# A transformer layer on one core: the first attention group's tiles filled on chip, and its shift rows written directly

## The chip, the cores and the metric

One core of a Trainium2 chip. The metric is the device time of one execution in microseconds (us). TensorE is PE in the profile, VectorE is DVE, ScalarE is ACT, GpSimd is POOL, SyncE is SP; PEld are TensorE's weight loads, and a q behind an engine (SPq, ACTq) marks its issues of DMAs.

## The reference

```python
# x: (2, 1024, 128) float32; 16 heads of two sub-heads each, HD = 4
def sdpa(qi, ki):
    s = jnp.einsum('bnhd,bmhd->bhnm', qi, ki) * scale
    p = jax.nn.softmax(s, axis=-1)
    return jnp.einsum('bhnm,bmhe->bhne', p, v)
o = sdpa(q0, k0) - lam * sdpa(q1, k1)        # differential attention
o = rms_norm(o, sub_norm_w) * (1.0 - LAMBDA_INIT)
...
x = x + attn_a(layernorm(x))    # the above, with w_qkv, w_proj, b_proj
x = x + ffn(layernorm(x))       # 64 experts, top 8 of them, and a shared one
x = x + attn_b(layernorm(x))    # attention among the 16 heads, summed over the sequence
x = x + ffn(layernorm(x))
```

## The kernel before

**Queries and keys.** The tokens are 4 chunks of 512 (`NCH`), two for each of the 2 batches. For a chunk VectorE and GpSimd make the norm, TensorE transposes, ScalarE copies the result to `XT`, and TensorE makes a tile of queries and one of keys. Each is split into three bf16 parts (`PARTS`): ScalarE copies the high part, VectorE subtracts it into `R1` (the remainder), ScalarE copies the middle part, VectorE subtracts again for the low part. A product of scores is one bf16 matmul over 32 rows: 6 pairs of parts (`Q_SLOTS`, `K_SLOTS`) of 4 elements, and 8 more rows of which three carry the shift of the softmax for each query against ones in the keys.

**The stacks.** SyncE writes these rows to DRAM (`q_stack`, `k_stack`), 14 transfers for each batch, and reads them back as tiles: a group is 4 sub-heads in 4 strips of 32 partitions, 16 groups in all (`NG`). `QB` and `KB` hold a group for the scores, `QA` and `KA` hold it for the max pass with the two halves of the keys in different strips. Each is double-buffered (u).

**The attention.** It runs in 256 quads (`NQ`), 16 for a group. A quad has four score matmuls, their four exps on ScalarE (`PR`, line 858), 16 matmuls of `PR` with the values (`VG`, line 1358) and two items of the max pass: two matmuls with 1024 keys (line 1294), and the maximum over them by VectorE (line 1065) into `NEGMAX`. The max pass runs `LEAD` = 12 quads ahead, so the first 24 items stand alone. After the 16 items of a half group GpSimd splits the 16 shifts of each partition into three bf16 parts (`SHP`, `shift_parts`), TensorE transposes them in the quad that is 3 before the half group's first scores, VectorE copies them to `SHT`, SyncE writes them to `shift_d` in DRAM and then in four transfers to `QB` (`shift_rows`). A score's bank is one of three (4 to 6), an item's two of four (0 to 3), bank 7 sums the values. `OTS` and `OSB` are the sums on their way out once in a half group.

**The weights of the experts.** `RAWU` and `RAWD` are loaded on ScalarE's queue, 2 MB each; ScalarE makes the high parts (`WUH`, `WDH`), GpSimd the low ones (`WUL`, `WDL`, line 628). The last quads overlap with the experts' beginning, after which eight passes (a chunk each, twice) over 16 groups of four experts and the shared one follow. `PR` lies over `PARTS`, so that the first exp waits for all writes of the stacks.

Each engine works through its own list in order; semaphores alone connect them. The order is written by hand.

## Time and profile before

| | |
|---|---|
| time, median of 3 runs | 1091.02 us (1089.59 to 1094.71) |
| the profiled execution | 1090.65 us |
| its span | 1088.8 us |
| VectorE busy | 959.6 us (88%) |
| TensorE busy | 1001.9 us (92%) |
| ScalarE busy | 890.0 us (82%) |
| GpSimd busy | 485.9 us (45%) |

The span goes from the first to the last instruction; the rest of the time lies around it. Busy times are sums over the span, and the stages differ: they are read by window. In brackets behind an instruction stands the idle time ahead of it and what ended it.

### The profile page before, as it was taken

The page shows a single profiled execution, that of the slowest core. Times are in us where ns is not written, and L with a number is a line of the kernel's source. Part 1 is how long each engine was busy: PE and PEld are TensorE (multiplying, and loading weights), DVE is VectorE, ACT ScalarE, POOL GpSimd, SP SyncE. Part 2 cuts the span into 40 slices and gives each one's busy share as a digit, 9 for nine tenths or more (in the row PEclk, how much of TensorE's full clock was granted, in tenths as well). Part 3 has the DMA queues.
Part 4 walks back from the last instruction along what each step waited for, and adds up shares of the span by engine and source line. Part 5 has one row for each costly group of instructions (what it writes and reads, how often), then busy time and mean ns, then how long its engine had stood idle before and what let it go on. Part 6 is the DMA issues. An engine that isn't in the chain of part 4 may idle for free.

```text
span 1088.8 us, 21671 instructions
## 1 busy us (share of the span) xinstructions
PE 1001.9 (92%) x8016; PEld 515.6 (47%) x8016; DVE 959.6 (88%) x1186; ACT 890.0 (82%) x1466; POOL 485.9 (45%) x893
## 2 busy tenths in 40 slices
PE   6389999999999999999999999999899999999998
PEld 3022222222222222222222236787677777777876
DVE  7799999999999999999999947798866988787665
ACT  5179999999999999999999987777775787678765
POOL 3363555455555544564556467342413431323331
PEclk9579999999999999999999999999999999999999
DMA  8911110111011101100110008575757466757763
GB/s 277 304 30 50 52 51 4 50 51 51 4 51 51 37 17 51 51 26 28 52 51 22 3 8 192 144 187 131 173 150 179 136 160 179 194 145 182 197 190 90
DMA packets 80473, 108.91 MB, mean 100 GB/s; under 512 B 23536, under 2 KB 33520, under 8 KB 80368
## 3 DMA queue, kind: packets, MB, share of 16 engines
q1 hardware_dynamic: 66336, 100.98, 34.4%
q10 hardware_dynamic: 14032, 6.55, 2.3%
q8 instruction: 64, 1.05, 0.4%
q14 instruction: 41, 0.34, 0.1%
HBM read 95.57 MB, written 11.93 MB: 99 GB/s over the span
## 4 chain that ended last, share of the span: by engine, by line
DVE 54%; PE 27%; ACT 7%; issue 6%; DMA 5%; POOL 1%; SPq 1%; ACTq 0%; DVEq 0%; POOLq 0%
DVE NEGMAX L1065 46%; PE PS L1456 7%; PE PS L1458 7%; PE PS L1457 7%; PE PS L1358 2%; DVE HF L1106 2%; DVE HL L1114 2%; ACT PR L858 2%; DMA GATE<-gate_d 1%; PE PS L1331 1%; ACT PS L955 1%; ACT HH L948 1%; ACT L955 1%; DVE ln_st L1000 1%; DMA shift_d<-SHT 1%
## 5 line engine op out<-in xcount | busy, mean ns | idle before, releaser
L1065 DVE TENSOR_REDUCE NEGMAX<-PS 128x1 f32<-128x1024 f32 x512 | 584.6, 1208 | 10.4 <-PE PS L1294 9.7
L858 ACT ACTIVATE PR<-PS 128x512 f32<-128x512 f32 x1024 | 538.9, 600 | 37.1 <-PE PS L1331 24.2
L1358 PE MATMUL PS<-PR,VG 128*32 128x256 f32 (+1 forms) x3840 | 321.3, 406 | 17.3 <-ACT PR L858 2.0
L1331 PE MATMUL PS<-QB,KB 32*128 32x512 bf16 x1024 | 260.1, 387 | 3.7 <-DMA QB<-shift_d 2.5
L1294 PE MATMUL PS<-KA,QA 32*128 32x512 bf16 x1024 | 204.3, 397 | 31.2 <-DVE NEGMAX L1065 22.4
L1106 DVE TENSOR_TENSOR HF<-PS,GATE 128x1024 f32<-128x1024 f32 x128 | 156.2, 1221 | 72.7 <-ACT PS L955 62.3
L1331 PEld LDWEIGHTS PS<-QB,KB 32*128 32x128 bf16 x1024 | 75.0, 91 | 239.8 <-ACT PR L858 137.4
L955 ACT ACTIVATE PS<-PS 128x1024 f32<-128x1024 f32 x128 | 129.2, 1010 | 71.5 <-PE PS L1458 70.9
L948 ACT ACTIVATE HH<-HF 128x1024 fp32r<-128x1024 f32 (+1 forms) x136 | 139.8, 1029 | 34.4 <-DVE HF L1106 32.6
L770 POOL TENSOR_TENSOR HL<-HF,HH 128x1024 fp32r<-128x1024 f32 (+1 forms) x32 | 69.2, 2162 | 165.8 <-ACT HH L948 165.8
L1358 PEld LDWEIGHTS PS<-PR,VG 128*32 128x32 f32 x3840 | 76.4, 108 | 130.7 <-issue 64.6
L1114 DVE TENSOR_TENSOR HL<-HF,HH 128x1024 fp32r<-128x1024 f32 x104 | 131.5, 1265 | 7.6 <-ACT HH L948 7.5
L1456 PE MATMUL PS<-XH,WUH 128*128 128x512 f32 x256 | 107.4, 420 | 0.0
L1456 PE MATMUL PS<-HH,WDH 128*128 128x512 f32 x256 | 103.1, 403 | 3.0 <-ACT YS L965 2.5
L1458 PE MATMUL PS<-HH,WDL 128*128 128x512 f32 x256 | 101.8, 398 | 0.0
L1457 PE MATMUL PS<-HL,WDH 128*128 128x512 f32 x256 | 101.3, 396 | 0.0
L1457 PE MATMUL PS<-XL,WUH 128*128 128x512 f32 x256 | 101.2, 395 | 0.0
L1458 PE MATMUL PS<-XH,WUL 128*128 128x512 f32 x256 | 101.0, 394 | 0.0
L676 POOL TENSOR_TENSOR ORC<-OSB,MINUS 128x16 f32<-128x16 f32 x32 | 93.2, 2911 | 3.3 <-DVE OSB L1091 0.9
L642 POOL TENSOR_TENSOR SHP<-NEGMAX,ZERO 128x16 bf16<-128x16 f32 x32 | 7.0, 218 | 167.5 <-DVE NEGMAX L1065 167.5
L1294 PEld LDWEIGHTS PS<-KA,QA 32*128 32x128 bf16 x1024 | 48.3, 91 | 59.4 <-DVE NEGMAX L1065 45.3
L1456 PEld LDWEIGHTS PS<-HH,WDH 128*128 128x128 f32 x256 | 48.6, 190 | 16.6 <-ACT YS L965 4.7
(186 smaller groups left out, 970.1 us busy)
## 6 DMA issues: line engine op xcount, KB each, us to landing
GATE<-gate_d SPq DMA_DIRECT2D x256, 256.0 KB, 4.1
QA<-q_stack SPq DMA_DIRECT2D x64, 128.0 KB, 2.6
QB<-q_stack SPq DMA_DIRECT2D x16, 256.0 KB, 2.9
KB<-k_stack SPq DMA_DIRECT2D x16, 256.0 KB, 3.0
KA<-k_stack SPq DMA_DIRECT2D x60, 64.0 KB, 2.4
q_stack<-PARTS SPq DMA_DIRECT2D x12, 256.0 KB, 4.4
k_stack<-PARTS SPq DMA_DIRECT2D x12, 256.0 KB, 4.6
RAWU<-in_L_ffn_W_up_dram ACTq DMA_DIRECT2D x4, 512.0 KB, 13.0
```

Of the source, the lines that this page charges most:

```text
L858: nc.scalar.activation(PR[:, s % PRING, r, :], PS[:, SCORE_BANK[n], :], ACT.Exp, scale=SCALE_A).then_inc(p_ready, 1)
L948: nc.scalar.activation(HH[:, k, 0:u, :], HF[:, f, 0:u, :], ACT.Copy).then_inc(hh_ok, 1)
L955: nc.scalar.activation(PS[:, z:z + 2, :], PS[:, z:z + 2, :], ACT.Silu).then_inc(silu_ok, 1)
L1065: nc.vector.tensor_reduce(NEGMAX[:, hs % 2, col:col + 1], PS[:, e:e + 2, :].rearrange("p b n -> p (b n)"), axis=AX_X, op=ALU.max, negate=T ...
L1106: nc.vector.tensor_tensor(HF[:, k, :, :], PS[:, z:z + 2, :], GATE[:, h % GSLOTS, :, :], op=ALU.mult).then_inc(hf_ok, 1)
L1114: nc.vector.tensor_tensor(HL[:, k, 0:u, :], HF[:, f, 0:u, :], HH[:, k, 0:u, :].bitcast(F32), op=ALU.subtract).then_inc(hl_ok, 1)
L1294: last = mm(PS[:, e + h, :], QA[lo:lo + STRIP, u, r // 2, nt * P:(nt + 1) * P], KA[lo:lo + STRIP, u, r // 2, :], start=True, stop=True)
L1331: mm(PS[:, SCORE_BANK[n], :], KB[strip, u, mt * P:(mt + 1) * P], QB[strip, u, half * BANK:(half + 1) * BANK], start=True, stop=True).then_ ...
L1358: last = mm(PS[STRIP * r:STRIP * (r + 1), 7, cols], VG[:, u, mt, r // 2, :], PR[:, s % PRING, r, cols], start=mt == 0, stop=mt == TB - 1 a ...
L1456: mm(dst, ah, bh, start=first, stop=False)
L1457: mm(dst, ah, bl, start=False, stop=False)
L1458: return mm(dst, al, bh, start=False, stop=last)
```

## The change

Group 0 of the attention no longer takes the way over DRAM: `QB` and `KB` are set to 0 and 1 by VectorE at the start, and 12 transfers (`first_rows`) write the parts of the first four sub-heads from `PARTS` into them. To make rows of one slot lie 8 partitions apart, the order of the 32 rows is now element by slot (`HD_A`, `SLOTS`). The max pass of group 0 reads `QB` and `KB`, both halves of the keys in one strip, and starts when these transfers have landed. The values' matmuls, before in one piece ahead of the max pass, stand one tile behind each of its items 1 to 16, and the centroids behind item 17; they use banks 4 to 6. The loads of `QA`/`KA` for group 0 are gone.

The first batch's parts are made in another order, with four buffers for the remainder and some low parts on GpSimd. TensorE runs 4 and 6 matmuls without use (`warm`) at the start. The writes of the stacks are 8 for a batch, those with several slots in one transfer. The small products of `lam` move from VectorE to GpSimd, X+BPROJ to its half group 3.

A shift row takes one transfer from `SHT` to `QB` (`shift_rows`); the transposed tile has a fourth, zero part, 64 partitions for 48. The load of `RAWU` goes to SyncE in 16 pieces behind the shift rows of groups 0 to 7, `WUH` is made in 8 pieces of 512 columns at quads 28, 44, ... 140, `WUL` in 8 pieces at half groups 6, 8, ... 20.

```diff
...
+SLOTS = STRIP // HD_A
+SHIFT_SLOT = SLOTS - 1
+STACK_WRITES = 16 * 2 * 4
+FIRST_LOADS = 16 * 2 * len(Q_SLOTS)
...
+A_LATE = A_ITEM["va", 0]
+def a_bank(n):
+    return n % 4 if n < A_LATE else 4 + (n - A_LATE) % 3
...
+UP_PIECES = 8
+UP_PARTS = 2 * UP_PIECES
+def up_piece(s):
+    k = (s - 28) // QPG
+    return k if s >= 28 and (s - 28) % QPG == 0 and k < UP_PIECES else None
...
+            load_x(0)
+            load_x(1)
+            sp.dma_start(WQKV[:], w_qkv.rearrange("(j p) c -> p j c", p=P)).then_inc(ld_w, 16)
+            sp.dma_start(WPRJ[:], w_proj).then_inc(ld_w, 16)
+            load_x(2)
+            load_x(3)
+            sp.wait_ge(const_ok, 2)
...
+                    step = places[1] - places[0] if len(places) > 1 else 1
+                    rows = stack[b * GPB:(b + 1) * GPB].rearrange("g r d c n -> (g r d) c n")[:, places[0]:places[-1] + 1:step, :]
+                    sp.dma_start(rows, src.unsqueeze(1).to_broadcast([P, len(places), SEQ])).then_inc(st_w[b], 16)
+            def first_rows(part):
+                for tile, j, slots in ((QB, 0, Q_SLOTS), (KB, 1, K_SLOTS)):
+                    for c in [c for c, a in enumerate(slots) if a == part]:
+                        sp.dma_start(tile[c:P:SLOTS, 0, :], PARTS[0:R * HD_A, part, j, 0:SEQ]).then_inc(first_ld, 16)
...
+            sp.wait_ge(first_set, 2)
+            for part, made in enumerate((qk_hi, qk_mid)):
+                sp.wait_ge(made, 2 * NCH // BATCH)
+                first_rows(part)
+            sp.wait_ge(qk_lo_pool, 2)
+            sp.wait_ge(qk_lo, 2)
+            first_rows(2)
+            for part in range(3):
+                write_parts(0, part)
+            fill_shift_rows(1)
+            for part, (made, n) in enumerate(((qk_hi, 2 * NCH), (qk_mid, 2 * NCH), (qk_lo_pool, 6))):
+                sp.wait_ge(made, n)
+                write_parts(1, part)
...
             sp.wait_ge(st_w[0], STACK_WRITES)
-            load_max(0, 0, False)
+            load_max(1, 1)
+            sp.wait_ge(const_ok, 3)
             sp.dma_start(RAWSU[:, 0:F], ws_up).then_inc(ld_exp, 16)
             sp.dma_start(RAWSD[0:F, :], ws_down).then_inc(ld_exp, 16)
-            fill_shift_rows(1)
-            write_stacks(1)
-            load_max(1, 1)
             sp.wait_ge(st_w[1], STACK_WRITES)
...
             def shift_rows(s, half):
                 u, hs = s % 2, 2 * s + half
+                if half == 0 and s:
+                    sp.wait_ge(sh_w, 16 * s)
                 sp.wait_ge(sht_ok, hs + 1)
-                sp.dma_start(shift_d[half].rearrange("a r (t n) -> (a r t) n", n=P), SHT[:, half, :]).then_inc(sh_w, 16)
-                sp.wait_ge(sh_w, 48 * s + 16 * (half + 2))
-                for r in range(R):
-                    lo = STRIP * r + SHIFT_ROW
-                    sp.dma_start(QB[lo:lo + 3, u, half * BANK:(half + 1) * BANK], shift_d[half, :, r, :]).then_inc(sh_r, 16)
+                sp.dma_start(QB[SHIFT_SLOT:P:SLOTS, u, half * BANK:(half + 1) * BANK], SHT[:, half, :]).then_inc(sh_r, 16)
...
                 for half in range(2):
                     shift_rows(s, half)
+                    if s < UP_PIECES:
+                        load_up(2 * s + half)
...
+            def low_part(c):
+                cols = slice(c * BANK, (c + 1) * BANK)
+                for j in range(2):
+                    n = D_ITEM["qk", j, c]
+                    pool.wait_ge(qk_mid, n + 1)
+                    nc.gpsimd.tensor_tensor(PARTS[:, 2, j, cols], R1[:, n % 4, :], PARTS[:, 1, j, cols], op=ALU.subtract).then_inc(qk_lo_pool, 1)
             for c in range(NCH):
                 root_of(("a", c))
+            for c in (0, 2, 3):
+                low_part(c)
...
+            def low_up(k):
+                cols = slice(k * BANK, (k + 1) * BANK)
+                low_weights(3 + k, WUL[:, cols], RAWU[:, cols], WUH[:, cols])
...
+            link(nc.gpsimd.memset(ZERO[:], 0.0))
+            link(nc.gpsimd.memset(SHP[:], 0.0))
             link(nc.gpsimd.memset(VG[:], 0.0))
             link(nc.gpsimd.memset(VG[:, :, :, :, VD:VD + 1], 1.0))
+            low_weights(0, WDL[:], RAWD[:], WDH[:])
+            pool.wait_ge(ld_mix, 16 * 9)
+            for j in range(2):
+                link(nc.gpsimd.tensor_tensor(lam_p[:, j, :], LAM[:, 2 * j, :], LAM[:, 2 * j + 1, :], op=ALU.mult))
+            link(nc.gpsimd.tensor_tensor(lam_p[:, :, 0:2], lam_p[:, :, 0:2], lam_p[:, :, 2:4], op=ALU.add))
+            nc.gpsimd.tensor_tensor(lam_s[:], lam_p[:, :, 0], lam_p[:, :, 1], op=ALU.add).then_inc(lam_in, 1)
+            link(nc.gpsimd.tensor_scalar(SUBW[:], SUBW[:], 1.0 - LAMBDA_INIT, None, ALU.mult))
+            shift_parts(0)
             values(0, 0)
             values(1, 1)
...
+                if hs == 3:
+                    pool.wait_ge(ln_xn, NCH)
+                    nc.gpsimd.tensor_tensor(X[:], X[:], BPROJ[:].unsqueeze(1).to_broadcast([P, NT, DIM]), op=ALU.add).then_inc(xb_ok, 1)
+                if hs >= 6 and hs % 2 == 0 and hs // 2 - 3 < UP_PIECES:
+                    low_up(hs // 2 - 3)
...
+            transposed(0)
+            high_part(0, 0)
+            transposed(1)
+            high_part(1, 0)
+            middle_part(0, 0)
+            high_part(0, 1)
+            middle_part(1, 0)
+            high_part(1, 1)
+            transposed(2)
+            middle_part(0, 1)
+            middle_part(1, 1)
+            transposed(3)
+            for c in range(2, NCH):
                 for j in range(2):
-                    n = D_ITEM["qk", j, c]
-                    act.wait_ge(d_full, n + 1)
-                    nc.scalar.activation(PARTS[:, 0, j, cols], PS[:, 4 + n % 4, :], ACT.Copy).then_inc(qk_hi, 1)
+                    high_part(j, c)
                 for j in range(2):
-                    n = D_ITEM["qk", j, c]
-                    act.wait_ge(qk_r1, n + 1)
-                    nc.scalar.activation(PARTS[:, 1, j, cols], R1[:, n % 2, :], ACT.Copy).then_inc(qk_mid, 1)
+                    middle_part(j, c)
+            act.wait_ge(ld_down, 16)
+            nc.scalar.activation(WDH[:], RAWD[:], ACT.Copy).then_inc(w_hi, 1)
             for c in range(NCH):
-                evac(("xT", c), XT[:, c * BANK:(c + 1) * BANK], lambda n: PS[:, n, :])
-                if c:
-                    high_and_middle(c - 1)
-            high_and_middle(NCH - 1)
-            for c in range(NCH):
-                b, h = c // 2, c % 2
-                evac(("va", c), VALL[:, b * GPB:(b + 1) * GPB, h * 4:(h + 1) * 4, :].rearrange("p g t v -> p t g v"),
-                     lambda n: PS[:, n, :].rearrange("p (t g v) -> p t g v", t=4, g=GPB))
+                values(c)
...
+            act.wait_ge(first_ld, FIRST_LOADS)
             for b in range(BATCH):
...
+            def high_up(k):
+                cols = slice(k * BANK, (k + 1) * BANK)
+                act.wait_ge(ld_up, 16 * UP_PARTS // UP_PIECES * (k + 1))
+                nc.scalar.activation(WUH[:, cols], RAWU[:, cols], ACT.Copy).then_inc(w_hi, 1)
...
+                if up_piece(s) is not None:
+                    high_up(up_piece(s))
...
+            def rest(j, c):
+                n = D_ITEM["qk", j, c]
+                dve.wait_ge(qk_hi, n + 1)
+                if n >= 4:
+                    dve.wait_ge(qk_mid, n - 3)
+                    if n < 6:
+                        dve.wait_ge(qk_lo_pool, n - 3)
+                    else:
+                        dve.wait_ge(qk_lo, n - 5)
+                nc.vector.tensor_tensor(R1[:, n % 4, :], PS[:, 4 + n % 4, :], PARTS[:, 0, j, c * BANK:(c + 1) * BANK],
+                                        op=ALU.subtract).then_inc(qk_r1, 1)
...
+            nc.vector.memset(QB[:, 0, :], 0.0).then_inc(first_set, 1)
+            nc.vector.memset(KB[:, 0, :], 1.0).then_inc(first_set, 1)
             for c in range(NCH):
                 dve.wait_ge(ld_x[c], 16)
                 stats(("a", c))
                 if c:
                     norm(("a", c - 1))
+            rest(0, 0)
+            rest(1, 0)
             norm(("a", NCH - 1))
-            for c in range(NCH):
-                rest_and_low(c)
-            dve.wait_ge(ld_mix, 16 * 9)
-            for j in range(2):
-                link(nc.vector.tensor_tensor(lam_p[:, j, :], LAM[:, 2 * j, :], LAM[:, 2 * j + 1, :], op=ALU.mult))
-            nc.vector.tensor_reduce(lam_s[:], lam_p[:], axis=AX_X, op=ALU.add).then_inc(lam_in, 1)
-            link(nc.vector.tensor_scalar(SUBW[:], SUBW[:], 1.0 - LAMBDA_INIT, None, ALU.mult))
+            rest(0, 1)
+            rest(1, 1)
+            low_part(0, 1)
+            low_part(1, 1)
...
+            for c in range(2, NCH):
+                rest(0, c)
+                rest(1, c)
...
-                nc.vector.tensor_copy(SHT[:, hs % 2, :], PS[0:3 * SHIFTS, SCORE_BANK[n], 0:P // 2].bitcast(BF16)).then_inc(sht_ok, 1)
+                    dve.wait_ge(sh_r, 16 * (hs - 1))
+                nc.vector.tensor_copy(SHT[:, hs % 2, :], PS[0:4 * SHIFTS, SCORE_BANK[n], 0:P // 2].bitcast(BF16)).then_inc(sht_ok, 1)
...
+            def warm(times):
+                for _ in range(times):
+                    mm(PS[:, 7, :], identb[:], ONES[:, 0:BANK], start=True, stop=True)
             pe.wait_ge(ident_ok, 1)
+            pe.wait_ge(identb_ok, 1)
+            pe.wait_ge(const_ok, 2)
+            warm(4)
...
+            def late_value(i):
+                c, j = divmod(i, 4)
+                n, t = A_ITEM["va", c], i
+                if i == 0:
+                    pe.wait_ge(qk_r1, 2 * NCH)
+                if j == 0 and n - A_LATE >= 3:
+                    pe.wait_ge(a_free, n - 2)
+                last = mm(PS[:, a_bank(n), j * P:(j + 1) * P], XT[:, t * P:(t + 1) * P], WT[:, 2, :], start=True, stop=True)
+                if j == 3:
+                    last.then_inc(a_full, 1)
+            def centroids():
+                n = A_ITEM["centT"]
+                pe.wait_ge(ld_b, 16 * 5)
+                pe.wait_ge(a_free, n - 2)
+                nc.tensor.transpose(PS[:, a_bank(n), 0:E], CENT[:], ident[0:E, 0:E])
+                nc.tensor.transpose(PS[:, a_bank(n), E:E + DIM], WB[:, 2, :], ident[:]).then_inc(a_full, 1)
+            warm(6)
+            transposed(0)
+            copied(0)
+            query_or_key(0, 0)
+            transposed(1)
+            query_or_key(1, 0)
+            copied(1)
+            query_or_key(0, 1)
+            query_or_key(1, 1)
+            transposed(2)
+            transposed(3)
+            for c in range(2, NCH):
+                copied(c)
+                query_or_key(0, c)
+                query_or_key(1, c)
+            pe.wait_ge(first_ld, FIRST_LOADS)
...
+                    if ga == 0:
+                        strip = slice(STRIP * r, STRIP * (r + 1))
+                        for h in range(2):
+                            last = mm(PS[:, e + h, :], QB[strip, 0, nt * P:(nt + 1) * P],
+                                      KB[strip, 0, h * BANK:(h + 1) * BANK], start=True, stop=True)
+                        last.then_inc(m_full, 1)
+                        if 1 <= it <= TOK // P:
+                            late_value(it - 1)
+                        elif it == TOK // P + 1:
+                            centroids()
+                        continue
...
+                    pe.wait_ge(sh_r, 16 * (s // TB + 1))
...
+                if s == 9 - LEAD:
+                    pe.wait_ge(a_free, len(A_ITEM))
...
```

## Rows read from the trace of the kernel before

**Rows 1.** The page: the chain by line, and the score matmuls in the table of groups.

```profile
DVE NEGMAX L1065 46%; PE PS L1456 7%; PE PS L1458 7%; PE PS L1457 7%; PE PS L1358 2%; DVE HF L1106 2%; DVE HL L1114 2%; ACT PR L858 2%; DMA GATE<-gate_d 1%; PE PS L1331 1%; ACT PS L955 1%; ACT HH L948 1%; ACT L955 1%; DVE ln_st L1000 1%; DMA shift_d<-SHT 1%
...
L1331 PE MATMUL PS<-QB,KB 32*128 32x512 bf16 x1024 | 260.1, 387 | 3.7 <-DMA QB<-shift_d 2.5
```

**Rows 2.** Table by stage: window; its length, busy time of each engine; granted clock, DMA share, GB/s.

```profile
36.60:62.00 25.40, 13.21 (x45) 2.37 (x45) 25.40 (x24) 4.11 (x4) 11.65 (x11) 0.50 0.90 276
62.00:70.00 8.00, 7.59 (x38) 1.25 (x36) 7.12 (x7) 5.12 (x10) 8.00 (x3) 0.51 0.00 1
...
670.00:1088.80 418.80, 395.38 (x1802) 316.24 (x1800) 327.59 (x509) 299.50 (x335) 135.86 (x123) 0.99 0.63 162
```

**Rows 3.** Timeline of the beginning: start, length over all instructions of the group, engine, line.

```profile
12.29 1.11 DVE L1012 TENSOR_SCALAR XC<-X,ln_mv,ln_inv 128x128 f32<-128x128 f32 x4
...
12.90 1.80 SPq L495 DMA_DIRECT2D EBIAS<-L_ffn_expert_biases_dram  x1
...
13.89 0.60 ACT L812 ACTIVATE PARTS<-PS 128x512 bf16<-128x512 f32 x1 [1.11 <-PE PS L1247]
...
15.69 1.28 DVE L1022 TENSOR_TENSOR SQ<-PS,PARTS 128x512 f32<-128x512 f32 x2
...
17.14 1.29 DVE L1027 TENSOR_TENSOR PARTS<-SQ,PARTS 128x512 bf16<-128x512 f32 x2 [0.17 <-ACT PARTS L816]
...
19.12 1.95 SPq L480 DMA_DIRECT2D q_stack<-PARTS  x3
...
23.02 3.73 PE L1253 MATMUL PS<-WT,XT 128*128 128x128 f32 x32
...
36.60 21.58 DVE L1065 TENSOR_REDUCE NEGMAX<-PS 128x1 f32<-128x1024 f32 x19 [7.66 <-PE PS L1294]
```

**Rows 4.** Timeline of VectorE, 60 to 690 us.

```profile
69.37 8.04 DVE L1065 TENSOR_REDUCE NEGMAX<-PS 128x1 f32<-128x1024 f32 x7 [0.88 <-PE PS L1294]
...
77.46 18.27 DVE L1065 TENSOR_REDUCE NEGMAX<-PS 128x1 f32<-128x1024 f32 x16
...
95.77 18.27 DVE L1065 TENSOR_REDUCE NEGMAX<-PS 128x1 f32<-128x1024 f32 x16
...
610.63 14.88 DVE L1065 TENSOR_REDUCE NEGMAX<-PS 128x1 f32<-128x1024 f32 x13
```

**Rows 5.** Chain of waits, 26 to 100 us: start, length, what.

```profile
26.35 2.75 DMA k_stack<-PARTS
...
31.20 4.62 DMA KA<-k_stack
```

**Rows 6.** Groups of instructions from 36 to 62 us.

```profile
L1294 PE MATMUL PS<-KA,QA 32*128 32x512 bf16 x48 | 14.0, 602 | 20.6 <-DVE NEGMAX L1065 12.2 <-DMA KA<-k_stack 8.3
...
L628 POOL TENSOR_TENSOR WDL<-RAWD,WDH 128x4096 fp32r<-128x4096 f32 x1 | 8.8, 8809 | 20.9 <-ACT WDH L839 20.9
```

**Rows 7.** Timeline from 55 to 80 us, SyncE's issues of the first shift rows.

```profile
59.72 1.20 SPq L536 DMA_DIRECT2D QB<-shift_d  x4
```

**Rows 8.** Tile SHT from 40 to 110 us: its writes to shift_d.

```profile
DMA to landing us min/median/max: 1.3/1.3/1.4
```

**Rows 9.** Tile PARTS up to 60 us: its writes to the stacks.

```profile
DMA to landing us min/median/max: 2.5/4.4/7.0
```

**Rows 10.** Timeline from 168 us: a score and a pair of the max pass.

```profile
168.05 0.39 PE L1331 MATMUL PS<-QB,KB 32*128 32x512 bf16 x1
168.05 0.39 PE L1294 MATMUL PS<-KA,QA 32*128 32x512 bf16 x2
```

**Rows 11.** Waits of TensorE, 60 to 680 us: in total, times, longest.

```profile
PE PS L1331 <- DMA QB<-shift_d: 2.5, 6, 0.9
```

**Rows 12.** Timeline of ScalarE, 124 to 164 us.

```profile
158.38 0.59 ACT L869 ACTIVATE OTS<-PS 128x512 f32<-128x512 f32 x1
158.86 1.58 ACT L858 ACTIVATE PR<-PS 128x512 f32<-128x512 f32 x3
```

**Rows 13.** Timeline of GpSimd, 100 to 180 us.

```profile
147.43 0.22 POOL L642 TENSOR_TENSOR SHP<-NEGMAX,ZERO 128x16 bf16<-128x16 f32 x1 [3.17 <-DVE NEGMAX L1065]
```

More of the change, by code:

```diff
@@ L365, in hybrid_layer @@
         OTS = sb("OTS", [P, 2, BANK], where=attn)
-        SHP = sb("SHP", [P, 2, 3 * SHIFTS], BF16, where=attn)
-        SHT = sb("SHT", [3 * SHIFTS, 2, P], BF16, where=attn)
+        SHP = sb("SHP", [P, 2, R, 4, SHIFTS // R], BF16, where=attn)
+        SHT = sb("SHT", [4 * SHIFTS, 2, P], BF16, where=attn)
         ZERO = sb("ZERO", [P, SHIFTS], where=attn)
@@ L495, in _, with load_max @@
             sp.dma_start(EBIAS[:], e_bias.partition_broadcast(P)).then_inc(ld_mix, 16)
-            write_stacks(0)
+            sp.wait_ge(first_set, 2)
[11 more added lines that the diff above has]
+                write_parts(1, part)
             def load_strips(stack, tile, u, g, there):
-                sp.dma_start(tile[:, u, :], stack[g].rearrange("r s n -> (r s) n")).then_inc(there, 16)
-            def load_max(u, g, keys=True):
+                sp.dma_start(tile[:, u, :], stack[g].rearrange("r d c n -> (r d c) n")).then_inc(there, 16)
+            def load_max(u, g):
                 for rp in range(R // 2):
@@ L839, in _ @@
-            nc.scalar.activation(WDH[:], RAWD[:], ACT.Copy).then_inc(w_hi, 1)
-            for part in range(4):
-                load_up(part)
-            act.wait_ge(ld_exp, 32)
-            act.wait_ge(ld_up, 16 * 4)
-            for dst, src in ((WUH, RAWU), (WSUH, RAWSU), (WSDH, RAWSD)):
-                nc.scalar.activation(dst[:], src[:], ACT.Copy).then_inc(w_hi, 1)
+            nc.scalar.activation(CT[:], PS[:, a_bank(n), 0:E], ACT.Copy)
+            nc.scalar.activation(WVT[:], PS[:, a_bank(n), E:E + DIM], ACT.Copy).then_inc(a_free, 1)
@@ L1231, in ring @@
                     pe.wait_ge(free, n - 3)
-                put((0 if items is A_ITEM else 4) + n % 4).then_inc(full, 1)
+                put(a_bank(n) if items is A_ITEM else 4 + n % 4).then_inc(full, 1)
             def transposes(tiles):
```

156 lines of the change are left out of this document (58 added, 98 removed).

## The prediction

> **What bounds the kernel now.** I read the page first. On the chain that ended last the row maxima (line 1065, VectorE) are 46%, far ahead of any other line [rows 1]. The table by stage then says where: from 36.6 us VectorE is busy without a gap, 25.40 of 25.40 us, while TensorE is busy 13.21 and granted 0.50 of its clock; behind 670 us TensorE is the busiest, 395.38 of 418.80 [rows 2]. So there are three stages: a beginning in which VectorE waits, then the attention at the pace of 512 maxima, then the experts at TensorE's pace. Nothing in the last two starts at a fixed time. Whatever the first maximum gains moves all that follows, unless it is lost again on the way.
>
> The timeline gives the first maximum at 36.60 and the pace of the lead, 21.58 us for 19 [rows 3]; in the steady part a block of 16 with the copy of the shifts takes 95.77-77.46 = 18.31 us, 1.13 for each maximum [rows 4]. The chain of waits says why it starts so late: the last write of a stack (issued 26.35, landed 29.10), then, from 31.20, KA landing at 35.82 [rows 5]. That is a round trip through DRAM after all the queries and keys of the first batch were ready.
>
> **The beginning, step by step.** The new kernel writes group 0's rows from PARTS straight into QB and KB.
> - High parts: the norm of chunk 2 ends at 12.29+1.11 = 13.40; VectorE then does the remainder of the first query tile, 1.28/2 = 0.64, to 14.05; ScalarE still owes a middle, a high, a middle and a high part at 0.60 each: 16.4 [rows 3]. Chunk 2's XT copy and two middle parts: 18.2. The last low part, 1.29/2 = 0.65 on VectorE: 18.9; the two on GpSimd are an eighth of the 8.81 us of WDL each, 1.1, from 14.7, and are done before that [rows 3, 6].
> - Issues: SyncE is free after EBIAS, 12.90+1.80 = 14.70 (the weight loads change places in front of it, their number doesn't change) [rows 3]. It issues 6 transfers from 16.4, 4 that need the middle parts, 2 that need the low ones. None of such a shape (16 partitions of 2 KB) is in the trace. The nearest are 1.20/4 = 0.30 for four of 3 rows and 1.95/3 = 0.65 for three of 128 [rows 3, 7]. I take 0.48: 16.4 + 12 x 0.48 = 22.2.
> - Landing: 1.3 for a small write of SHT [rows 8], 2.5 / 4.4 / 7.0 for the writes of PARTS [rows 9]. I take 2.5, as the queue still holds earlier loads: 24.7. From KA landed to the first maximum passed 36.60-35.82 = 0.8: the first maximum is at 25.5.
> - Bounds: with 0.65 and 4.4 it is 24.2+4.4+0.8 = 29.4. With 0.30 and 1.3 the rows would be there at 21.5, but VectorE is not free: ScalarE has seven more copies at 0.60 up to the high part of chunk 3's keys, with some 0.5 of waiting 22.9, and VectorE's remainder ends at 23.6. So 23.7.
> Gain: 36.6-25.5 = **11.1 us** (7.2 to 12.9). The added memsets of QB and KB lie ahead of X's arrival, where VectorE waits anyway; the 10 warming matmuls lie where TensorE waits for weights and the first norm. If that cover were gone, the ten would cost some 0.4 each, 4 in all.
>
> **The lead.** Now TensorE has more to do between two maxima. A pair of score matmuls took 602 ns at half clock [rows 6]; a single one 387 at full clock [rows 1]. The difference, 0.215, is what 512 columns gain from 1.2 to 2.4 GHz, so the stream itself is 0.43 and 0.215, and the rest is latency. The pair of before lies in two different strips of 32 partitions; for group 0 both halves use one strip. If they still ran side by side it would cost nothing; if in turn, one stream more, 0.43 or 0.215. I take the second, because a score in one strip and a pair in two others start at the same 168.05 and all end in 0.39 [rows 10]: side by side is what separate strips give, and the trace shows none in one strip. The Trainium skill, TensorEngine Tiling (Array Packing), section Tiling Modes, says that different tiles run their matmuls in parallel, which leaves two in the same tile to run in turn; by the pair's row alone this term is zero, by that rule it is one stream a pair. No row here shows it.
> A value tile is two passes of 3.73/32 = 0.117 at full clock, 0.233 at half [rows 3]. An item then occupies TensorE 2 x 0.43 + 2 x 0.233 = 1.32 at half clock against VectorE's 1.13: 0.19 lost in each of 16 items, 3.0 at most. At full clock it is 0.66, nothing. TensorE so loaded should be granted full speed, as it was after 62 to 70 (busy 7.59 of 8 at 0.51 [rows 2]; nearly all later score matmuls are at the 387 ns of full clock [rows 1]); I take 5 items at half clock, less the half microsecond of buffering: 0.5.
> Before, VectorE lost 0.88 when the scores began at half clock [rows 4]. The last 7 items of the lead carry no values, so the clock may fall again before them; group 0's last 8 items then cost two streams a quad in quads 0 to 3, 4 x 2 x 0.43 = 3.4 more. At full clock the 0.88 comes back. I take 1.0 more than before. Lead in all: **1.5 lost** (0.9 gained to 6.4 lost).
>
> **Shifts.** The detour over shift_d goes: one issue and one landing instead of two landings and four more issues on SyncE. The first scores of a half group need them some 4.5 us after the copy of SHT (from quad -3 to quad 0 lie five maxima, 5.65, and TensorE runs one ahead). Mostly they were there: the blocks from 77.46 to 610.63 are 29 x 18.31 = 531.0 in 533.2, so 2.1 us too long, and TensorE waited six times, 2.5 in all, for these rows [rows 4, 11]. Gain between 0 and 2.1; I take **1.7**. The transposed tile grows from 48 to 64 partitions, which a copy's time does not follow.
>
> **Work moved under the steady state.** WUH and WUL leave the lead, where they were hidden. In eight pieces they lie between exps: each 512 columns on ScalarE, like the OTS copy's 0.59 [rows 12]. That copy stands in every half group and the maxima keep their 18.27 [rows 4]; ScalarE makes three exps in 1.58 behind it [rows 12], 0.53 each, so 17.0 for 32, with both copies 17.9 of 18.3. A piece of 0.59 every second half group is caught up within two. Nothing to 0.59 each; I take 0.1: **0.8 lost** (0 to 4.7). What stands behind it is the next quad's exps, then TensorE's bank. GpSimd's share is 1.1 every 36 us, while it idles 3.17 before the fuller of its half groups' next shift [rows 13]; X+BPROJ (2048 columns, by WDL's 4096 in 8.81 some 4.4 us) falls in an emptier one: nothing, and if that cover were gone the shift would be late by what exceeds it. RAWU's 16 small loads come behind a shift's issue on SyncE, ahead of nothing due within 10 us.
> The stack writes are 8 transfers a batch for 14, with the same bytes. ScalarE's first exp (PR lies over PARTS) and SyncE's first shift wait for all of them. From 22.2: 3+1+3 MB and QA/KA. At the 276 GB/s of the lead's row [rows 2] 7.3 MB take 26.6 us, to 49; the first shift is due at 25.5+21.6+0.2 = 47.3 and its rows are needed 4.5 later, at 51.8. It fits if nothing else is in the way; nothing taken.
>
> **Sum.** -11.1+1.5-1.7+0.8 = -10.5. On the profiled execution's 1090.65 (span 1088.8 and 1.85 around it) this gives 1080.15; it lies 0.4 below the median of the runs, so for that **1080.5**.
>
> **Rivals.**
> 1. The clock stays at half through the lead and the first quads, with one strip in turn: the lead loses 6.4 instead of 1.5. For it: 0.50 in all of 36.6 to 62 [rows 2]. Against: TensorE would be nearly full. [...] -11.1+6.4-1.7+0.8 = -5.6: 1085.4. Chance 0.14.
> 2. The stack writes are late. At 200 GB/s instead of 276 they land at 58.7, 7 us after need: -3.5, 1087.5. Against: the new writes compete with no RAWU load. Chance 0.08.
> 3. Slower: the direct write into 16 spread partitions (64 pieces of 256 bytes) takes longer to land than the chain it replaces. It decides from some 4.4 us of landing; at 4.9 each of 32 half groups loses 0.5, 16 us against 10.5 gained: 1096.5. Against: 1.3 for the same SHT rows going to DRAM [rows 8]. Chance 0.05.
> 4. The change doesn't do what it says: the early start waits for the stacks all the same, in ScalarE's or SyncE's queue, and only the shifts gain: 1089 to 1091. Chance 0.04.
> 5. Early rows at the lower bound, clock full throughout: -12.9-0.9-2.1: 1075. Chance 0.07.
> The forecast, 1077 to 1084.5, has 0.62. A measurement here tells 0.5%, 5.5 us. Faster (below 1085.6): forecast 0.62, rival 5 0.07, 0.10 of 1 and 0.02 of 2 with a smaller delay: 0.81. Slower: rival 3 and a hundredth for stalls not thought of: 0.06. Same: the rest, 0.13. Range: 1075.5 to 1087.0; it leaves out rivals 3 and 4 and the edge of 5.
>
> **What would show it.** First maximum between 24 and 27 us, ended by a DMA into QB or KB and not by VectorE's remainders. Item matmuls of group 0 near 0.6 (full) or 1.0 us (half) a pair. Maxima 1.13 apart through items 0 to 31. The first exp about 53. Blocks of 16 maxima at 18.31 without late ones, no TensorE wait on QB's shift rows, and none longer where a WUH piece stands (quads 28, 44, ...). The stage behind attention as long as before. The prediction is wrong if the first maximum comes after 30, if the first exp waits for a store of PARTS, or if every block grows.

## The result, and the profile after

The changed kernel takes 1095.93 us (median of 13 runs, 1091.87 to 1101.96) against 1091.02 for the kernel before in 13 runs beside them (1088.15 to 1095.60): the ratio is 1.0051, with an interval of 1.0032 to 1.0070. 1080.5 was forecast. The change made the kernel some 5 us slower. The profiled execution took 1095.64 us, with a span of 1093.8.

The page, the chain by line, and the score matmuls in its table of groups (compare [rows 1]):

```profile
DVE NEGMAX L1133 41%; PE PS L1567 6%; PE PS L1569 6%; PE PS L1568 6%; ACT PR L915 4%; PE PS L1469 4%; PE PS L1391 2%; PE PS L1442 2%; DVE HF L1174 2%; DVE HL L1182 1%; PE PS L1351 1%; ACT HH L1007 1%; DMA GATE<-gate_d 1%; ACT PS L1014 1%; PE PS L1305 1%
...
L1442 PE MATMUL PS<-QB,KB 32*128 32x512 bf16 x1024 | 263.0, 389 | 0.8
```

Two lines of TensorE are new on the chain: 1391, the items of group 0, and 1351, the value tiles between them. The maxima fell from 46% to 41%. So for a stretch TensorE, not VectorE, sets the pace. The last two columns of the score row say the rest: 0.8 us of idle time ahead of them, where it was 3.7, and no wait for shift rows among its causes.

The timeline of VectorE (the first maxima, four of the lead, the first copy of SHT, quads 0 to 3, the second copy, a steady block, the fourth copy; compare [rows 3, 4]):

```profile
26.86 3.58 DVE L1133 TENSOR_REDUCE NEGMAX<-PS 128x1 f32<-128x1024 f32 x3 [1.56 <-PE PS L1391]
...
30.90 1.23 DVE L1133 TENSOR_REDUCE NEGMAX<-PS 128x1 f32<-128x1024 f32 x1 [0.47 <-PE PS L1391]
32.59 1.22 DVE L1133 TENSOR_REDUCE NEGMAX<-PS 128x1 f32<-128x1024 f32 x1 [0.46 <-PE PS L1391]
...
57.87 0.21 DVE L1146 COPY SHT<-PS 64x128 bf16<-64x128 bf16 x1
...
70.20 1.23 DVE L1133 TENSOR_REDUCE NEGMAX<-PS 128x1 f32<-128x1024 f32 x1 [1.61 <-PE PS L1391]
72.18 1.23 DVE L1133 TENSOR_REDUCE NEGMAX<-PS 128x1 f32<-128x1024 f32 x1 [0.75 <-PE PS L1391]
...
81.97 0.22 DVE L1146 COPY SHT<-PS 64x128 bf16<-64x128 bf16 x1 [0.21 <-PE PS L1412]
...
118.76 18.27 DVE L1133 TENSOR_REDUCE NEGMAX<-PS 128x1 f32<-128x1024 f32 x16
137.28 0.22 DVE L1146 COPY SHT<-PS 64x128 bf16<-64x128 bf16 x1 [0.25 <-PE PS L1412]
```

The first maximum stands at 26.86 for 36.60. But the maxima of the lead then come 32.59-30.90 = 1.69 us apart, not 1.13, each with a wait of 0.46 for line 1391; in quads 0 to 3 they are 1.98 apart. TensorE's own timeline shows what one item is:

```profile
25.79 1.04 PE L1391 MATMUL PS<-KB,QB 32*128 32x512 bf16 x4 [3.24 <-DMA KB<-PARTS]
...
31.52 1.03 PE L1391 MATMUL PS<-KB,QB 32*128 32x512 bf16 x2
32.48 0.80 PE L1351 MATMUL PS<-WT,XT 128*128 128x128 f32 x2
33.20 1.03 PE L1391 MATMUL PS<-KB,QB 32*128 32x512 bf16 x2
```

A pair from its start to the tile's start is 0.96, a value tile 0.72 to 0.73, and no idle time stands between them. The table by stage gives the clock (columns as in [rows 2]; here busy PE, PEld, DVE, ACT, POOL, then the clock):

```profile
26.00:36.00 10.00, 9.41 (x25) 3.28 (x21) 7.29 (x7) 4.07 (x2) 9.46 (x7) 0.50 1.03 379
36.00:46.00 10.00, 10.00 (x25) 3.63 (x25) 7.31 (x6) 0.60 (x1) 3.44 (x6) 0.50 1.00 353
46.00:56.00 10.00, 9.52 (x25) 3.71 (x26) 7.35 (x6) 1.98 (x7) 1.44 (x7) 0.50 0.25 71
...
70.00:76.00 6.00, 6.00 (x37) 1.00 (x36) 3.67 (x3) 3.32 (x7) 0.00 (x0) 0.50 0.00 0
76.00:82.00 6.00, 5.90 (x54) 1.51 (x57) 4.93 (x5) 4.41 (x9) 0.89 (x4) 0.67 0.01 4
```

From 26 to 56 us TensorE is busy 9.4 to 10.0 of 10 us and is granted half of its clock (1.2 GHz) all the same; it stays at half to past 76 us. Between starts on the two timelines, the difference of the spans splits up without a rest:

| stretch | before | after | difference |
|---|---|---|---|
| start to first maximum | 36.60 | 26.86 | -9.74 |
| to the first copy of SHT | 21.51 | 31.01 | +9.50 |
| to the second copy | 19.22 | 24.10 | +4.88 |
| to the 31st copy (610.50; 616.13) | 533.17 | 534.16 | +0.99 |
| to the end of the span | 478.30 | 477.67 | -0.63 |
| span | 1088.8 | 1093.8 | +5.0 |

So the early start was gained nearly as forecast and lost behind it, in the lead and in the first quads.

### The profile page after: what moved, and what is told of

Same layout as the page of the kernel before. It is cut to its first block, busy times and chain, and to the rows that moved or that the text cites. A ratio compares the mean times of both kernels' runs of the same rounds, so it can differ in the third digit from the quotient of the medians.

```text
span 1093.8 us, 21589 instructions
## 1 busy us (share of the span) xinstructions
PE 1025.4 (94%) x8026; PEld 521.2 (48%) x8026; DVE 961.2 (88%) x1178; ACT 890.2 (81%) x1473; POOL 496.6 (45%) x912
## 4 chain that ended last, share of the span: by engine, by line
DVE 46%; PE 31%; ACT 9%; issue 7%; POOL 3%; DMA 3%; SPq 1%; DVEq 0%; ACTq 0%; POOLq 0%
DVE NEGMAX L1133 41%; PE PS L1567 6%; PE PS L1569 6%; PE PS L1568 6%; ACT PR L915 4%; PE PS L1469 4%; PE PS L1391 2%; PE PS L1442 2%; DVE HF L1174 2%; DVE HL L1182 1%; PE PS L1351 1%; ACT HH L1007 1%; DMA GATE<-gate_d 1%; ACT PS L1014 1%; PE PS L1305 1%
## 5 line engine op out<-in xcount | busy, mean ns | idle before, releaser
L1442 PE MATMUL PS<-QB,KB 32*128 32x512 bf16 x1024 | 263.0, 389 | 0.8
L1403 PE MATMUL PS<-KA,QA 32*128 32x512 bf16 x960 | 186.6, 385 | 11.8 <-DVE NEGMAX L1133 11.8
L1403 PEld LDWEIGHTS PS<-KA,QA 32*128 32x128 bf16 x960 | 45.1, 91 | 27.8 <-DVE NEGMAX L1133 20.9
```

What stands on the lines that cost most here:

```text
L1403: last = mm(PS[:, e + h, :], QA[lo:lo + STRIP, u, r // 2, nt * P:(nt + 1) * P], KA[lo:lo + STRIP, u, r // 2, :], start=True, stop=True)
L1442: mm(PS[:, SCORE_BANK[n], :], KB[strip, u, mt * P:(mt + 1) * P], QB[strip, u, half * BANK:(half + 1) * BANK], start=True, stop=True).then_ ...
```

## The experiments

Each ratio is against the kernel before, run beside it. Where not said otherwise, an edit is made to the changed kernel, and only its main lines are shown (`...` stands for the others). The rest behind the 31st copy differs between profiled executions by more than some of these edits are worth (last section), so each run is also read up to a copy of SHT.

**First question: why the clock stays at half.** TensorE waits 3.24 us ahead of its first item. Fourteen matmuls without use fill that gap.

```diff
                 query_or_key(1, c)
+            warm(14, 3)
             pe.wait_ge(first_ld, FIRST_LOADS)
```

> The changed kernel plus 14 matmuls without use (bank 3) between the last query/key tile and the wait for the first rows, so that TensorE does not idle 3.2 us ahead of item 0. Theory A (the clock fell in that gap and, once at half, the lead's own work cannot raise it): item 0 starts at full clock and the lead stays there, items 1.13 apart instead of 1.69, up to 9 us gained by the first copy of SHT. Theory B (it is the lead's work itself that does not hold the clock, whatever it was before): full clock for a few items only, then 1.69 again, 1 to 3 us gained.

1096.90 (1.0047, 1.0027 to 1.0067). VectorE's timeline has its first items at the old pace:

```profile
27.02 6.88 DVE L1133 TENSOR_REDUCE NEGMAX<-PS 128x1 f32<-128x1024 f32 x6 [1.14 <-PE PS L1392]
...
56.23 0.20 DVE L1146 COPY SHT<-PS 64x128 bf16<-64x128 bf16 x1
...
76.90 0.21 DVE L1146 COPY SHT<-PS 64x128 bf16<-64x128 bf16 x1
```

They are 1.15 apart to 34 us, then 1.69 again. The table by stage:

```profile
26.00:36.00 10.00, 8.55 (x30) 3.10 (x29) 8.10 (x7) 4.64 (x3) 9.44 (x7) 0.79 1.03 377
36.00:46.00 10.00, 10.00 (x24) 3.65 (x24) 7.35 (x6) 1.19 (x2) 3.99 (x6) 0.50 1.02 366
...
64.00:70.00 6.00, 6.00 (x31) 0.87 (x29) 4.17 (x4) 3.38 (x8) 0.00 (x0) 0.55 0.00 0
70.00:76.00 6.00, 5.84 (x73) 1.69 (x72) 5.89 (x6) 5.88 (x12) 0.88 (x4) 1.00 0.01 3
```

The gap is not what keeps the clock at half: while TensorE did the lead's work, the clock fell from full within 8 us of the first item. The filled gap brought the first copy of SHT 1.8 us nearer to the first maximum (29.21 for 31.01). More came behind it: the clock was back by 70 us, some 10 us earlier than in the changed kernel, though the code of the first quads is the same, and the stretch to the second copy is 20.67 for 24.10. The 31st copy stands at 611.11 for 616.13, 5.0 us earlier. The time does not show it: behind that copy this execution took 482.1 us for 477.7.

**Second: which of the lead's two loads costs what.** All value tiles before the first item, as in the kernel before, in banks 2 to 5 (the centroids in 6), with ScalarE's copies of them and of the centroids ahead of WDH:

```diff
...
+            for c in range(NCH):
...
+                for i in range(4):
+                    late_value(4 * c + i)
...
+            centroids()
             pe.wait_ge(first_ld, FIRST_LOADS)
...
-                        if 1 <= it <= TOK // P:
-                            late_value(it - 1)
...
```

> The changed kernel with the 16 value tiles and the centroids made ahead of the max pass (banks 2 to 6) instead of one behind each item; ScalarE copies the first two before its last middle parts. Theory (TensorE is the bound in the lead, 1.03 for a pair and 0.66 more for a value tile at half clock): items fall from 1.69 to 1.13 to 1.18 apart, the first copy of SHT comes 8 to 9 us earlier, the first maximum at 26.9 to 28; total 7 to 9 us below the changed kernel. Rival (the period is set by the handshake with VectorE over two bank pairs, each value tile is hidden): items stay near 1.69.

1087.98 (0.9964, 0.9946 to 0.9983). The first maximum did not move, and 19 maxima take 22.25 us:

```profile
26.68 22.25 DVE L1136 TENSOR_REDUCE NEGMAX<-PS 128x1 f32<-128x1024 f32 x19 [1.86 <-PE PS L1398]
49.10 0.22 DVE L1149 COPY SHT<-PS 64x128 bf16<-64x128 bf16 x1 [0.17 <-PE PS L1415]
...
63.43 1.23 DVE L1136 TENSOR_REDUCE NEGMAX<-PS 128x1 f32<-128x1024 f32 x1 [0.75 <-PE PS L1398]
```

From first maximum to first copy it is 22.42 for 31.01: 8.6 of the 9.5 us come back. The clock is no better for it:

```profile
26.00:36.00 10.00, 6.56 (x19) 0.94 (x18) 9.32 (x9) 4.75 (x5) 8.27 (x7) 0.74 1.03 379
```

It fell in this window and stood at 0.50 to the end of the lead, so pairs alone do not hold it either. In quads 0 to 3 the items are 1.98 apart as in the changed kernel, so that loss is not the tiles'.

From item 6 the second half of the keys is read from copies of QB and KB, turned by two strips, which four transfers on ScalarE's queue make:

```diff
+            act.wait_ge(first_ld, FIRST_LOADS)
+            for lo in (0, 64):
+                act.dma_start(QA[lo:lo + 64, 0, 0, :], QB[64 - lo:P - lo, 0, :]).then_inc(turned, 16)
+                act.dma_start(KA[lo:lo + 64, 0, 0, :], KB[64 - lo:P - lo, 0, BANK:SEQ]).then_inc(turned, 16)
...
```

> The changed kernel, with the second half of the keys and the queries copied once more, turned by 64 partitions, into free room of KA and QA; from item 6 of group 0 on, the two matmuls of an item use two strips. Theory (a pair in one strip runs in turn, 0.43 more at half clock): a pair takes 0.60 instead of 1.03, items 1.26 apart instead of 1.69 while value tiles lie between, and in quads 0 to 3 items 1.5 apart instead of 1.97; 5 to 9 us gained in all. Rival (they run side by side already and 1.03 is the cost of the tile switch from the value matmuls): no change.

1090.16 (0.9990, 0.9971 to 1.0009).

```profile
36.10 15.16 DVE L1137 TENSOR_REDUCE NEGMAX<-PS 128x1 f32<-128x1024 f32 x12 [2.24 <-PE PS L1402]
...
64.25 8.13 DVE L1137 TENSOR_REDUCE NEGMAX<-PS 128x1 f32<-128x1024 f32 x7 [0.89 <-PE PS L1402]
72.30 0.21 DVE L1150 COPY SHT<-PS 64x128 bf16<-64x128 bf16 x1
```

A pair in two strips takes 0.60 where one in one strip takes 1.03, at the same half clock: in one strip the two halves ran in turn. The Trainium skill, TensorEngine Tiling (Array Packing), section Tiling Modes, says that different tiles run their matmuls in parallel, and the 0.60 agrees; that two in the same tile take turns is what the prediction concluded from it, and the 1.03 shows it. Items are now 1.26 apart with their value tiles; VectorE waited 2.24 ahead of item 6, as TensorE waited for the turned copies; and quads 0 to 3 have one stall, of 0.89, like the kernel before: 19.33 between the copies of SHT for 24.10. The clock was back at some 65 us here (0.93 in 64 to 70), so a part of this can be the earlier clock, as in the first run.

**Third: the blocks with a piece of WUH.** The piece moves from the quad ahead of the shift's transposition into the one behind it.

```diff
-    k = (s - 28) // QPG
-    return k if s >= 28 and (s - 28) % QPG == 0 and k < UP_PIECES else None
+    k = (s - 29) // QPG
+    return k if s >= 29 and (s - 29) % QPG == 0 and k < UP_PIECES else None
```

> The changed kernel with the eight WUH pieces one quad later (quads 29, 45, ...), behind the quad that holds the shift's transposition instead of ahead of it. Theory (the piece delays ScalarE, thus the bank, thus the transposed shift tile for which VectorE waits in order without a buffer): the 0.33 us that eight blocks of 16 maxima lose falls to under 0.1, 2 to 2.7 us gained in all. Rival (the loss is ScalarE's throughput, or GpSimd's piece): it stays at 0.33 in each.

1095.78 (1.0019, 0.9997 to 1.0041; the medians alone give 1.0037), and the time alone decides nothing. The timeline does: from 82.18 to 613.76 are 531.58 us, 29 x 18.33. The waits of 0.25 ahead of every second copy (at 137.28 above), which made those blocks 18.65 long, are gone, some 2.6 us. So it is the place of the piece and not ScalarE's load; nor is it GpSimd's share, whose first piece of WUL comes at 186.34, behind the first of these waits.

**The three edits together** (value tiles ahead, two strips from item 6, the pieces of WUH a quad later):

> The changed kernel with three edits: values and centroids ahead of the max pass, the second half of the keys in a turned copy from item 6 on, WUH pieces one quad later. By what each gave alone: first copy of SHT at 48.5 to 49.5 (lead at 1.13 to 1.17 an item after the start at 26.7), quads 0 to 3 as in the kernel before (one stall near 0.9), second copy at 68 to 69 against 77.3 before, blocks at 18.32 throughout. Then the end at 1079 to 1082, 1% below the kernel before. Rival: what the start gains comes back as another stall behind the lead (stack writes, SyncE), 1086 or more.

1084.26 (0.9938, 0.9912 to 0.9965), above the range expected. VectorE waited 3.13 ahead of item 6 for the turned copies, and the first copy of SHT stands at 52.00. That wait is what the next edit, made to this kernel, removes, by using the turned copies from item 10:

```diff
-                        if it == 6:
+                        if it == 10:
...
-                            if h and it >= 6:
+                            if h and it >= 10:
```

> The kernel with the three edits, but the turned copies are first read by item 10 and not 6, which waited 3.1 us for them. Theory: items 6 to 9 pass in one strip at 1.17, item 10 at 38.9 finds the copies landed (36.7), the second copy of SHT comes 2.5 to 3 us earlier than 71.6, total 1081 to 1082. Rival: the lead's gain is lost again at the first scores, which wait for the stack writes: no change.

1081.87 (0.9912, 0.9894 to 0.9931), the fastest of the kernels without fillers (below).

```profile
27.59 21.92 DVE L1140 TENSOR_REDUCE NEGMAX<-PS 128x1 f32<-128x1024 f32 x19 [1.85 <-PE PS L1409]
49.42 0.20 DVE L1153 COPY SHT<-PS 64x128 bf16<-64x128 bf16 x1
...
69.25 0.21 DVE L1153 COPY SHT<-PS 64x128 bf16<-64x128 bf16 x1
...
600.64 0.21 DVE L1153 COPY SHT<-PS 64x128 bf16<-64x128 bf16 x1
```

The 31st copy stands at 600.64 for 610.50 in the kernel before, 9.9 us earlier, and the median is 10.2 lower. That is about the 10.5 forecast for the change, once the early start is not paid back; it is not the same sum, since the start gave 9.0 here and not 11.1.

**Fourth: what holds the clock.** Matmuls without use over all 128 rows (`identb` with 512 columns of KB), from here on called fillers, a number of them behind each item:

```diff
+                        if 0 <= it < 24:
+                            for _ in range(2):
+                                mm(PS[:, 7, :], identb[:], KB[:, 0, 0:BANK], start=True, stop=True)
```

The first try has one filler behind items 6 to 23 of the kernel with three edits:

> The kernel with the three edits, and behind each of items 6 to 23 one matmul without use over all 128 rows (512 columns, bf16, into bank 7), which TensorE has the time for. Theory (the grant answers to how much of the array works, and 32-row matmuls count little: the lead as it stands never raises it): the clock rises within the lead, at 35 to 45 us, and quads 0 to 3 pass at full clock without a stall, up to 1 us gained. Rival (the gaps between items are what keeps it down, or the fillers are still too little): half clock to the end of the lead; the fillers then cost up to 0.3 us an item.

1087.31 (0.9954, 0.9932 to 0.9975). The clock had fallen ahead of the first filler (0.75 in 26 to 36) and stays at half:

```profile
46.00:56.00 10.00, 9.56 (x26) 1.81 (x25) 9.61 (x11) 0.71 (x3) 3.04 (x12) 0.50 0.47 126
```

Then two and three behind items 0 to 23 of the fastest kernel:

> The last kernel with two matmuls without use (128 rows, 512 columns) behind each of items 0 to 23. TensorE starts the lead at full clock. Theory (the grant follows how densely the whole array is fed): at full clock an item and two fillers are 0.65 to 0.86 of stream in 1.13; if that is too little, the clock falls at 31 to 34 as without them, an item then costs 1.3 to 1.5 and the lead loses 4 to 8 us; if it is enough, full clock through the lead, no stall at quads 0 to 3, 1 to 2 us gained. Rival (the clock answers only to gaps in which TensorE waits): it stays full in either case.

> The same with three fillers an item: 0.86 to 1.08 of stream in 1.13 at full clock. Theory: the clock stays full from the start through quads 0 to 3, no stall there, items 1.13 to 1.17 apart, up to 2 us below the kernel without fillers. If the clock falls all the same, an item costs 1.7 to 2.1 and the lead loses 15 us or more, and density is not what counts.

1082.20 (0.9904, 0.9873 to 0.9936) and 1083.15 (0.9925, 0.9909 to 0.9942). With two:

```profile
36.00:46.00 10.00, 8.81 (x36) 1.91 (x36) 10.00 (x9) 1.97 (x1) 7.89 (x1) 1.00 1.03 381
46.00:56.00 10.00, 8.26 (x39) 2.00 (x38) 9.94 (x11) 0.91 (x4) 4.47 (x16) 1.00 0.63 198
...
60.00:64.00 4.00, 4.00 (x36) 0.84 (x36) 3.60 (x4) 2.23 (x6) 0.00 (x0) 0.58 0.02 4
```

Full clock at 8.26 busy of 10, where the changed kernel had half at 10.00. The DMA share, 1.03, is no lower, so the transfers of the lead do not hold the clock down. The last filler ended at 55.4 us, and from some 60 us the clock was at half for some 3 us. The stretch to the second copy is 18.90 for 19.83 without fillers. The time is still that of the kernel without fillers, within the intervals: at half clock its items already fit under VectorE's 1.13, and a faster TensorE finds nothing to shorten in the lead. Three fillers are one too many: from first maximum to first copy it is 23.29 for 21.65 with two.

The same two fillers, but from item 10 only, so that they come after the clock has fallen (one profiled execution):

```diff
-                        if 0 <= it < 24:
+                        if 10 <= it < 24:
```

> The kernel with the three edits (turned copies from item 10), two fillers an item, but only from item 10 on, when the clock has fallen. Theory A (density alone decides: at half clock two fillers and a pair fill TensorE, which the hardware takes as busy): the clock rises some us behind item 10, items first 1.5 apart, then 1.13. Theory B (what holds the clock is not enough to raise it, or what counts is the work done and not the time busy): it stays at half to the first quads, items 1.5 apart, 5 us lost against the kernel with two fillers from item 0.

```profile
46.00:56.00 10.00, 10.00 (x29) 1.76 (x29) 7.38 (x8) 0.71 (x3) 3.27 (x13) 0.50 0.46 135
56.00:60.00 4.00, 4.00 (x14) 0.60 (x13) 3.72 (x4) 0.00 (x0) 0.00 (x0) 0.50 0.14 33
```

The clock does not come back in the 20 us of fillers. Items are 1.51 apart, and the copies of SHT stand at 53.92 and 74.92, for 49.42 and 69.25 without fillers. What holds a full clock did not restore one here, and the added work at half clock was paid for.

Last, the change as it is, with the gap filled and two fillers behind items 1 to 23, to price the clock in the change itself:

```diff
+            warm(14, 3)
             pe.wait_ge(first_ld, FIRST_LOADS)
...
+                        if 1 <= it < 24:
+                            for _ in range(2):
+                                mm(PS[:, 7, :], identb[:], KB[:, 0, 0:BANK], start=True, stop=True)
```

> The change as it stands (values behind the items, one strip, WUH pieces at 28), plus 14 matmuls ahead of the first rows' wait and two fillers behind each of items 1 to 23. Theory (the lead's loss is the half clock; at full clock pair, value tile and fillers are 1.09 of stream in 1.13): the clock stays full through the lead, the first copy of SHT comes at 48 to 50 instead of 57.9, 6 to 9 us below the change in all, although TensorE has more work than in the change. Rival (one strip and the value tiles bind TensorE by latency whatever the clock): items 1.3 or more apart, at most 4 us gained.

1093.28 (1.0014, 0.9996 to 1.0032). The clock is 1.00 from 26 to 60 us. TensorE's timeline:

```profile
35.09 0.60 PE L1392 MATMUL PS<-KB,QB 32*128 32x512 bf16 x2
35.62 0.49 PE L1351 MATMUL PS<-WT,XT 128*128 128x128 f32 x2
35.95 0.59 PE L1401 MATMUL PS<-KB,identb 128*128 128x512 bf16 x2
36.47 0.60 PE L1392 MATMUL PS<-KB,QB 32*128 32x512 bf16 x2
```

At full clock a pair in one strip takes 0.53 and a value tile 0.33, 0.86 in all: under 1.13. The items are 1.38 apart, and the fillers' 0.52 is what lies above that 0.86. So the first copy came at 52.89 and not at 48 to 50 as expected, and 5.0 of the lead's 9.5 us came back. That the change's lead runs at VectorE's pace when its clock is full is shown by the first run, whose first items, without fillers, were 1.15 apart. The clock fell at some 62 us, 4 us behind the last filler, and the items of quads 0 to 3 were 1.98 apart again; the second copy stands at 76.27 for 81.97.

**Fifth: the shifts alone**, written directly, in the kernel before; then with X+BPROJ moved to half group 3 as well.

```diff
...
-                sp.dma_start(shift_d[half].rearrange("a r (t n) -> (a r t) n", n=P), SHT[:, half, :]).then_inc(sh_w, 16)
-                sp.wait_ge(sh_w, 48 * s + 16 * (half + 2))
-                for r in range(R):
-                    lo = STRIP * r + SHIFT_ROW
-                    sp.dma_start(QB[lo:lo + 3, u, half * BANK:(half + 1) * BANK], shift_d[half, :, r, :]).then_inc(sh_r, 16)
+                sp.dma_start(QB[SHIFT_SLOT:P:SLOTS, u, half * BANK:(half + 1) * BANK], SHT[:, half, :]).then_inc(sh_r, 16)
...
```

> The kernel before with the direct shift rows alone (rows in order element by slot, 64-partition transposed tile, one transfer from SHT to QB); everything of the beginning as before. Theory (the gain is the late blocks and nothing else): no block over 18.35, TensorE waits for no shift row, the stretch between the second and the last copy of SHT is 531.3 us instead of 533.2, total 2 us below before. Rival (a write into 16 spread partitions lands later than the chain it replaces): longer blocks, more waits, slower.

1092.33 (0.9992, 0.9974 to 1.0009). The late blocks are gone (97.98 to 611.13: 28 x 18.33), but the second copy waits:

```profile
78.81 0.22 DVE L1077 COPY SHT<-PS 64x128 bf16<-64x128 bf16 x1 [1.57 <-PE PS L1302]
```

GpSimd makes WUL (8.86 from 62.53) and X+BPROJ (4.54 from 72.79) ahead of the second shift, which comes at 77.28. In the kernel before that addition ended at 75.44, just as the shift was due. WUL began 1.9 later here (62.53 for 60.67) because ScalarE waited longer for RAWU to land; whether the edit has a part in that, one profiled execution does not show.

```diff
+                if hs == 3:
...
+                    nc.gpsimd.tensor_tensor(X[:], X[:], BPROJ[:].unsqueeze(1).to_broadcast([P, NT, DIM]), op=ALU.add).then_inc(xb_ok, 1)
```

> The kernel before with the direct shift rows and X+BPROJ moved from ahead of GpSimd's second shift to half group 3, as the change has it. Theory (the direct rows alone lost their gain because GpSimd came 1.6 us late to the second shift behind WUL and this addition): no wait of VectorE before the second copy of SHT, no drop of the clock at 80, the late blocks gone as well, 2 us below the kernel before. Rival: as without the move, no difference.

1090.60 (0.9989, 0.9976 to 1.0001). The wait is gone: the copies from the second (77.06) to the 31st (608.51) take 531.45 us for 533.17, 1.7 less. The time of neither kernel is told apart from that of the kernel before; the gain is read from the timeline.

## Why the prediction was wrong, step by step

- **The beginning** held: 9.7 us gained for 11.1, and the wait of the first item was ended by the DMA into KB. The 1.4 us are four differences: SyncE began at 16.80 for 16.4 (0.4 later); an issue took 0.62 us and not 0.48 (12 in 7.5 us: 1.7 later); the first item began 1.5 us behind the last issue (25.79 for 24.33), where 2.5 were taken (1.0 earlier); and the first maximum 1.07 behind that for 0.8 (0.3 later). In the lower bound the rows are there at 16.4 + 12 x 0.30 + 1.3 = 21.3, not 21.5; the bound does not rest on it.
- **The lead is the step that failed**: "TensorE so loaded should be granted full speed ... I take 5 items at half clock". It was granted half for the whole lead and the first quads, 26 to 76 us. The ground given for it was the rise after 62 to 70 in the kernel before; what followed there was scores, exps and value sums together, not the lead's mixture. The first run here and the ones with fillers show that busy time was the wrong thing to read: 10.00 of 10 us at half, 8.26 of 10 at full.
- **The price at half clock was too small as well**: rival 1 has the right mechanism (chance 0.14) and loses 6.4 in the lead, where 9.50+4.88 = 14.4 were lost. An item was worked out at 1.32 and took 1.69: the pair 0.96 for 0.86, the value tile 0.73 for 0.47. Over 16 items 16 x 0.56 = 9.0. The tile's price came from 32 in a row [rows 3]; behind a pair of 32 rows it costs more, at full clock too (0.33 for 0.23, with a filler behind it). Quads 0 to 3 lost 4.9 for the 3.4 of the bound.
- **One strip is one after the other**: right, and shown by the pair's 0.60 against 1.03. By itself it cost little in the lead (value tiles ahead: 1.17 an item). The 4.9 of quads 0 to 3, where scores share TensorE with it, are gone with two strips (19.33), but it takes the half clock as well: with one strip and the clock back by 70 us the same stretch took 20.67, 1.45 more than before.
- **Shifts**: right. 1.7 taken; in the changed kernel 533.17 - (534.16 - 8 x 0.33) = 1.65, and alone, without a new wait, 1.7. The writes landed in 1.8 us; rival 3 fell, and that the measured time lies near its 1096.5 is chance.
- **WUH pieces**: 0.8 taken, 2.6 lost, within the bounds. The prediction asked what lies behind a piece and named the next exps, but not that VectorE reads the shift's transposed tile in its own order: a score bank freed 0.6 later delays this tile, the copy waits 0.25, and the maxima behind the copy with it.
- **Stack writes**: not late; rivals 2 and 4 fell. No wait for a store of PARTS stood ahead of the scores or the first exp.
- **Sum with the measured terms** (start, lead and first quads, shifts, WUH pieces, the rest behind the 31st copy): -9.7+14.4-1.65+2.6-0.6 = +5.0.

## What to carry to other kernels

Before work is put under an engine that has room, price the item at the clock that the stretch has now, with each tile's price from a place where it alternates with its new neighbours; a lead that fits even at half clock (a pair of 0.60 in two strips or 0.96 in one, against VectorE's 1.13) does not depend on it. Two matmuls of 32 rows that are to run at once need different strips. What moves to ScalarE or GpSimd belongs behind the tile that the pacing engine reads next, not ahead of it.
